# A conditional residual block, item by item: the reaction in a PSUM bank, the identity behind the transposition, and a new order of every engine's slot

## The chip, the cores and the metric

The kernel runs on one core of one Trainium2 chip. The metric is the device time of one execution in microseconds (us). Engines are named as the profile names them: PE is TensorE (PEld its weight loads), DVE VectorE, ACT ScalarE, POOL GpSimd, SP SyncE, which only issues DMAs here.

## The reference

There are 128 items, each a float32 matrix of S = 128 rows and D = 512 columns, and a few numbers per item: a kind (3), a language (10), a category (64), zX, zY, zR. Four residual steps follow one another:

```
scores = tanh(x @ W1 + b1) @ v                      # A = 128 hidden columns
p  = softmax(scores where mask(kind) else -1e30)    # 128 x 128, cnt = allowed columns per row
x1 = x + (p @ x) / cnt
h  = relu(x1 @ W1[lang] + b1[lang]) @ W2[lang] + b2[lang]
x2 = x1 + layernorm(x1 + h) * gamma[lang] + beta[lang]
x3 = x2 + zX*lap_columns(x2) + zY*lap_rows(x2) + zR*x2*(1 - x2)
out = x3 + x3 @ W[cat] + b[cat]
```

`lap` is the second difference with reflected ends, along the columns or along the rows.

## The kernel before, in words

Tables are made first: the items are sorted by category on the chip, so that a category's weights (1 MB, `w3s`, a ring of two places) are fetched only where it changes. Of the 128 fetches 55 are real; for the others the DMA is skipped. Small tables of integers per item (category, is it fresh, place of its weights, item, language, kind) lie in one row, `all_params`; an engine fetches such words into registers with a TENSOR_LOAD (`load_params`, L235).

Then the main loop. Each engine has its own program, written out by hand as slots: slot s does one step of item s, the next step of item s-1, and so on, up to five items apart. Engines meet only at semaphores (`wait_ge`), and each engine takes its instructions in the written order. Every tile of an item has a ring of two. The steps of one item:

- ACT's queue loads the item twice, transposed (`xts`, L565) and plain (`xs`, L572). PE projects the transposed one (`attn_project` L361, `adapter_project` L383); ACT applies tanh (L549); PE makes the scores and adds the mask (L372, L373).
- DVE takes the row maximum (L679), ACT the exponentials and their sum (L502). DVE makes the scale and, at L713, `mix = probs * scale + identity`, so that the residual x1 = x + pooled is one product. PE transposes mix into PSUM (L389), ACT copies it out (`move_mixT`, L524).
- PE: `adapter_hidden` L395, `pool` L402 (x1, into `ps_pool`), ACT: relu L530, PE: `adapter_up` L411 into `ps_adapt`. DVE adds b2 and beta to x1 (L771, L777), sums, centers and normalizes (L686, L692, L722, L746) with ACT's sum of squares (L517) and POOL's inverse deviation (`inverse_std`, L865). L746 writes x2.
- SP copies x2 shifted by one row up and down, with single rows for the reflected ends, through six DMAs inside the on-chip memory (`shift_rows`, L281). POOL adds the two (`sum_rows`, L885) and adds the column neighbours (`sum_columns`, L873; the two ends by ACT, L557).
- Reaction: ACT computes c0 - zR*x2 into the tile `react` (L539), POOL multiplies it by x2 (L879), DVE adds zX times the column sums (`add_columns`, L754) and zY times the row sums (`add_rows`, L764), which gives x3.
- PE transposes x3 in four parts (L419), ACT copies it (L496), PE multiplies by the category's weights (`category`, L429: four blocks of two passes) into `ps_out`, of which there are two banks. POOL adds x3 to the bias (`add_b3`, L892), DVE adds the two (`result`, L739), SP stores it (L272). SP also fetches the weights (L259) and the bias (L267).

PE's slot holds pool, scores, category (its first block, then adapter_up, then the other three), mix_transpose, both projections of the next item, x3_transpose and adapter_hidden. POOL's slot is sum_rows, sum_columns, add_b3, react_times_x2, inverse_std.

Of the kernel before, what the change touches and what calls it, by code (L numbers as in the profile page):

```python
# [12 lines left out]
P = 128  # L13
# [3 lines left out]
CAT, FRESH, WSLOT, ITEM, LANG, KIND, NPARAM = 0, 1, 2, 3, 4, 5, 6  # L17
# [47 lines left out]
def cond_residual_kernel(nc, x, xT, ids, cols, w1a,  # L65
# [22 lines left out]
    with ctx:  # L88
# [71 lines left out]
        react = sb("react", [P, 2, D])  # L160
# [14 lines left out]
        ps_out = [pb("ps_out0"), pb("ps_out1")]  # L175
# [3 lines left out]
        ps_wide = ps_out[0]  # L179
        b2_banks = [ps_out[1], bank_scores]  # L180
# [62 lines left out]
        def _(sp):  # L243
# [31 lines left out]
            def shift_rows(i):  # L275
                q = i.ring(2)
                sp.wait_ge(x2_ready, i.upto())
                for to, at, rows, source in ((below, 0, P - 2, 1), (above, 2, P - 2, 1),
                                             (below, P - 2, 1, P - 1), (below, P - 1, 1, P - 2),
                                             (above, 0, 1, 1), (above, 1, 1, 0)):  # L280
                    sp.dma_start(to[at:at + rows, q], x2[source:source + rows, q]).then_inc(shift_in[q], 16)  # L281

            def slot(s):
# [10 lines left out]
            run_slots(slot, 0, B + 1)  # L294
# [6 lines left out]
        def _(pe):  # L301
# [74 lines left out]
            def adapter_project(s, lang):  # L376
# [3 lines left out]
                if s.is_at_least(2):  # L380
                    pe.wait_ge(relu_ready, s.upto(2))
# [9 lines left out]
            def adapter_hidden(f):  # L391
                if (f + 1).inside(B):
                    pe.wait_ge(xw_ready, (f + 1).upto())
# [28 lines left out]
            def category(j, wslot, ks):  # L422
                if 0 in ks:
                    pe.wait_ge(x3T_ready, j.upto())
                    pe.wait_ge(w3_in[j.ring(2)], j.dma())
                    if j.is_at_least(2):
                        pe.wait_ge(res_ready, j.upto(2))
                for k in ks:
                    mm = pe.matmul(ps_out[j.ring(2)][:, :], x3T[:, j.ring(2), k * P:(k + 1) * P],  # L429
# [3 lines left out]

            def slot(s):
                h, j = s - 1, s - 4
                if h.inside(B):
                    pool(h)
                if s.inside(B):
                    kind, = load_params(pe, KIND, 1, s)
                if j.inside(B):  # L440
                    wslot, = load_params(pe, WSLOT, 1, j)
                if h.inside(B):
                    lang_m1, = load_params(pe, LANG, 1, h)
                if s.inside(B):
                    attn_scores(s, kind)
                if j.inside(B):
                    category(j, wslot, range(0, 1))
                if h.inside(B):
                    adapter_up(h, lang_m1)
                if j.inside(B):  # L450
                    category(j, wslot, range(1, K))
                if (s + 1).inside(B):
                    lang_p1, = load_params(pe, LANG, 1, s + 1)
                if s.inside(B):
                    mix_transpose(s)
                if (s + 1).is_first:
                    attn_project(s + 1)
                    adapter_project(s + 1, lang_p1)
                elif (s + 1).inside(B):
                    adapter_project(s + 1, lang_p1)  # L460
                    attn_project(s + 1)
                if (s - 3).inside(B):
                    x3_transpose(s - 3)
                if s.inside(B):
                    adapter_hidden(s)

            run_slots(slot, -1, B + 3)


        @block.scalar  # L470
        def _(act):
# [48 lines left out]
            def move_mixT(b):  # L520
                act.wait_ge(mixT_mm, b.upto())
                if b.is_at_least(2):
                    act.wait_ge(pool_mm, b.upto(2))
# [423 lines left out]
```

## Time and profile before

| | us |
|---|---|
| three runs | 1098.07, 1097.93, 1093.10 |
| median | 1097.93 |
| the profiled execution, its own time | 1097.21 |
| its span, from the first to the last instruction | 1095.4 |

| engine | busy us | share of the span |
|---|---|---|
| PE | 1055.9 | 96% |
| DVE | 956.5 | 87% |
| POOL | 710.9 | 65% |
| ACT | 504.8 | 46% |

The granted PE clock was 0.998 of full speed. The DMAs moved 268.92 MB, 246 GB/s on average; queue 1 (SP's) took 58.7% of the engines' time and queue 10 (ACT's) 20.4%. A busy share is an average over the run, so it doesn't say what ended a slot; the chain of waits does that for one stretch. "Idle before" of a row is the time that the engine stood still ahead of it, with the engine or DMA that released it.

### The profile page before, as it was taken

How to read it: one execution, taken by the hardware profiler on the slowest of the kernel's cores; microseconds unless marked ns; L12 is line 12 of the kernel's file. 1: busy time of each engine (PE TensorE's matmuls, PEld its weight loads, DVE VectorE, ACT ScalarE, POOL GpSimd, SP SyncE). 2: the span in 40 equal slices, each digit the busy share in tenths (PEclk: the TensorE clock that was granted, in tenths of full speed). 3: DMA queues.
4: the chain of work that ended last, by engine and by line, in shares of the span. 5: the costliest groups of instructions: out<-in, count | busy, mean ns of one | idle time of the engine just before them, and what ended most of it. 6: DMA issues, size and time to landing. Idle time of an engine off the chain costs nothing.

```text
span 1095.4 us, 23744 instructions
## 1 busy us (share of the span) xinstructions
PE 1055.9 (96%) x4912; PEld 656.8 (60%) x4912; DVE 956.5 (87%) x1962; ACT 504.8 (46%) x1422; POOL 710.9 (65%) x665
## 2 busy tenths in 40 slices
PE   6799999999999999999999999999999999999996
PEld 3565666656655656666665566665666565566562
DVE  5799989989989899999888888989898898999994
ACT  3444444444444444445444444444444444444441
POOL 3467667666666676667657666767665766667765
PEclk9999999999999999999999999999999999999999
DMA  8688798678779977876786868887879788897873
GB/s 346 199 260 236 247 293 244 203 250 254 245 230 288 298 239 237 246 229 203 228 266 193 265 198 255 269 266 235 269 241 262 228 268 237 288 276 226 244 241 115
DMA packets 134732, 268.92 MB, mean 246 GB/s; under 512 B 29139, under 2 KB 29157, under 8 KB 127173
## 3 DMA queue, kind: packets, MB, share of 16 engines
q1 hardware_dynamic: 97476, 199.83, 58.7%
q10 hardware_dynamic: 37120, 67.58, 20.4%
q8 instruction: 49, 0.80, 0.3%
q14 instruction: 87, 0.70, 0.2%
HBM read 243.21 MB, written 33.55 MB: 253 GB/s over the span
## 4 chain that ended last, share of the span: by engine, by line
PE 54%; issue 21%; POOL 17%; DVE 6%; DVEq 1%; ACTq 0%; ACT 0%; DMA 0%; POOLq 0%; SPq 0%
PE ps_out L429 23%; POOL b_wide L892 6%; PE ps_adapt L411 6%; PE bank_hidden L383 6%; PE ps_attn L361 6%; PE ps_pool L402 6%; POOL neighbours L873 4%; POOL react L879 3%; PE ps_x3T L419 3%; POOL rstd L865 2%; DVE x L764 2%; PE bank_scores L372 2%; PE bank_hidden L395 1%; DVE res L739 1%; POOL above L885 1%
## 5 line engine op out<-in xcount | busy, mean ns | idle before, releaser
L429 PE MATMUL ps_out<-w3s,x3T 128*128 x1024 | 490.1, 601 | 2.3 <-ACT x3T L496 2.3
L885 POOL TENSOR_TENSOR above<-above,below 128x512 f32<-128x512 f32 x128 | 166.7, 1303 | 226.7 <-DMA above<-x 223.7
L429 PEld LDWEIGHTS ps_out<-w3s,x3T 128*128 128x128 f32 x1024 | 185.1, 191 | 190.6 <-issue 188.7
L764 DVE SCALAR_TENSOR_TENSOR x<-above,wide_rows,react 128x512 f32<-128x512 f32 x128 | 189.5, 1481 | 13.9 <-POOL above L885 12.5
L879 POOL TENSOR_TENSOR react<-react,x 128x512 f32<-128x512 f32 x128 | 175.5, 1371 | 2.4 <-ACT react L539 2.4
L892 POOL TENSOR_TENSOR b_wide<-b_wide,x 128x512 f32<-128x512 f32 x128 | 173.1, 1352 | 1.7 <-DMA b_wide<-in_b 1.7
L865 POOL TENSOR_TENSOR rstd<-var_eps,minus_half 128x1 f32<-128x1 f32 x128 | 70.2, 549 | 132.0 <-DVE var_eps L731 131.9
L517 ACT ACTIVATE square_junk<-ps_adapt,neg_mean 128x512 f32<-128x512 f32 x128 | 88.1, 688 | 139.1 <-DVE neg_mean L692 139.1
L411 PE MATMUL ps_adapt<-w_all,hid 128*128 x256 | 133.0, 601 | 12.6 <-DVE x L746 12.2
L383 PEld LDWEIGHTS bank_hidden<-w_all,xts 128*128 128x128 f32 x1024 | 124.4, 192 | 28.4 <-issue 26.4
L383 PE MATMUL bank_hidden<-w_all,xts 128*128 x1024 | 137.2, 277 | 0.0
L873 POOL TENSOR_TENSOR neighbours<-x 128x510 f32<-128x510 f32 x128 | 133.4, 1042 | 3.6 <-DVE x L746 3.6
L361 PE MATMUL ps_attn<-xts,w_attn 128*128 128x128 f32 x1024 | 135.3, 275 | 0.3 <-issue 0.3
L402 PE MATMUL ps_pool<-xs,mixT 128*128 128x512 f32 x256 | 131.0, 594 | 0.0
L361 PEld LDWEIGHTS ps_attn<-xts,w_attn 128*128 128x128 f32 x1024 | 124.6, 192 | 0.5 <-issue 0.5
L739 DVE TENSOR_TENSOR res<-ps_out,b_wide 128x512 f32<-128x512 f32 x128 | 87.2, 682 | 36.1 <-POOL b_wide L892 26.0
L713 DVE SCALAR_TENSOR_TENSOR mix<-probs,scale,ident 128x128 f32<-128x128 f32 x128 | 108.7, 849 | 0.3 <-issue 0.3
L686 DVE SCALAR_TENSOR_TENSOR ps_adapt<-ps_adapt,x_b 128x512 f32<-128x512 f32 x128 | 89.4, 698 | 17.0 <-PE ps_adapt L411 16.1
L539 ACT ACTIVATE react<-x,c_t,nzr_t 128x512 f32<-128x512 f32 x128 | 102.8, 803 | 2.8 <-DVE x L746 2.8
L502 ACT ACTIVATE probs<-bank_scores,neg_max 128x128 f32<-128x128 f32 x128 | 47.1, 368 | 118.3 <-DVE neg_max L679 118.0
L754 DVE SCALAR_TENSOR_TENSOR react<-neighbours,wide_rows,react 128x512 f32<-128x512 f32 x128 | 96.8, 756 | 0.5 <-POOL react L879 0.5
L722 DVE SCALAR_TENSOR_TENSOR ps_adapt<-ps_adapt,neg_mean,gamma_wide 128x512 f32<-128x512 f32 x128 | 95.5, 746 | 0.1
(111 smaller groups left out, 1281.3 us busy)
## 6 DMA issues: line engine op xcount, KB each, us to landing
w3s<-in_w SPq DMA_DIRECT2D x128, 1024.0 KB
xts<-in_xT ACTq DMA_DIRECT2D x128, 256.0 KB, 4.7
xs<-in_x ACTq DMA_DIRECT2D x128, 256.0 KB, 5.0
b_wide<-in_b SPq DMA_DIRECT2D x128, 256.0 KB, 4.2
out_x<-res SPq DMA_DIRECT2D x128, 256.0 KB, 3.4
below<-x SPq DMA_DIRECT2D x128, 252.0 KB
above<-x SPq DMA_DIRECT2D x128, 252.0 KB
below<-x SPq DMA_DIRECT2D x256, 2.0 KB
```

The source lines that it names most:

```text
L361: mm = pe.matmul(ps_attn, w1_attn[:, k * A:(k + 1) * A], xts[:, r, k, :], start=(k == 0), stop=(k == K - 1))
L383: mm = pe.matmul(ps_xw, xts[:, s.ring(2), k, :], w1_all[:, bass.ds(lang * (K * A) + k * A, A)], start=(k == 0), stop=(k == K - 1))
L402: pe.matmul(ps_pool[:, :], mixT[:, d.ring(2), :], xs[:, d.ring(2), :], start=True, stop=True).then_inc(pool_mm, 1)
L411: pe.matmul(ps_adapt[:, :], hid[:, g.ring(2), :], w2_all[:, bass.ds(lang * D, D)], start=True, stop=True).then_inc(adapt_mm, 1)
L429: mm = pe.matmul(ps_out[j.ring(2)][:, :], x3T[:, j.ring(2), k * P:(k + 1) * P], w3s[:, bass.ds(wslot * (K * D) + k * D, D)], start=(k == 0 ...
L539: nc.scalar.activation(react[:, h.ring(2), :], x2[:, h.ring(2), :], ACT.Identity, bias=c0_t[:, bass.ds(h.n, 1)], scale=nzr_t[:, bass.ds(h. ...
L713: nc.vector.scalar_tensor_tensor(mix[:, p, :], probs[:, p, :], scale[:, p:p + 1], ident[:, :], ALU.mult, ALU.add).then_inc(mix_ready, 1)
L764: nc.vector.scalar_tensor_tensor(x3[:, q, :], above[:, q, :], zy_t[:, bass.ds(i.n, 1)], react[:, q, :], ALU.mult, ALU.add).then_inc(x3_rea ...
L873: nc.gpsimd.tensor_tensor(neighbours[:, q, 1:D - 1], x2[:, q, 0:D - 2], x2[:, q, 2:D], ALU.add).then_inc(neighbours_ready, 1)
L879: nc.gpsimd.tensor_tensor(react[:, q, :], react[:, q, :], x2[:, q, :], ALU.mult).then_inc(react_x2_ready, 1)
L885: nc.gpsimd.tensor_tensor(above[:, q, :], above[:, q, :], below[:, q, :], ALU.add).then_inc(rows_ready, 1)
L892: nc.gpsimd.tensor_tensor(b3_wide[:, q, :], b3_wide[:, q, :], x3[:, q, :], ALU.add).then_inc(x3_b3_ready, 1)
```

## The change

- The reaction is computed in a PSUM bank, `ps_react`, in place of the two-deep tile `react` in on-chip memory. Its product with x2 moves from POOL to DVE.
- `mix = probs * scale` without the identity is now made by ACT (`scale_rows`); the identity is added by DVE while it copies the transposed mix out of PSUM (`add_identity`), which ACT did.
- `ps_out` is one bank, where there were two; the other is `ps_react`. So `category` waits for the `result` of the item before, and ACT's `reaction` for x3 of the item before.
- SP fetches four words per item at once (is it fresh, place, category, item) and keeps them for the later steps; PE, ACT and DVE fetch two at once. The order of the words in the table is changed to suit.
- Every engine's slot has a new order. SP: shift_rows, load_b3 of the item before, store, load_w3. POOL: inverse_std, add_b3, sum_columns, sum_rows.

```diff
-        react = sb("react", [P, 2, D])
-        ps_out = [pb("ps_out0"), pb("ps_out1")]
+        ps_react = pb("ps_react")
+        ps_out = pb("ps_out")
...
 SP
             def slot(s):
                 if s.inside(B):
-                    cat, fresh, wslot = load_params(sp, CAT, 3, s)
+                    words[(s).n] = load_params(sp, FRESH, 4, s)
                     shift_rows(s)
-                    load_w3(s, cat, fresh, wslot)
-                if (s - 2).inside(B):
-                    item_m2, = load_params(sp, ITEM, 1, s - 2)
-                    store(s - 2, item_m2)
-                if s.inside(B):
-                    load_b3(s, cat)
+                if (s - 1).inside(B):
+                    load_b3(s - 1, words[(s - 1).n][2])
+                if (s - 3).inside(B):
+                    store(s - 3, words[(s - 3).n][3])
+                if s.inside(B):
+                    load_w3(s, words[(s).n][2], words[(s).n][0], words[(s).n][1])
...
 ACT
-            def move_mixT(b):
-                act.wait_ge(mixT_mm, b.upto())
-                nc.scalar.activation(mixT[:, b.ring(2), :], ps_mixT, ACT.Copy).then_inc(mixT_ready, 1)
+            def scale_rows(b):
+                act.wait_ge(scale_ready, b.upto())
+                nc.scalar.activation(mix[:, p, :], probs[:, p, :], ACT.Copy, scale=scale[:, p:p + 1]
+                                     ).then_inc(mix_ready, 1)
...
 ACT's slot now: load_x(s-1), scale_rows(s-2), words and load_xT(s), variance(s-3), attn_tanh(s-1),
 relu(s-2), reaction(s-4), exponentials(s-1), move_x3T(s-5), column_ends(s-3), move_xw(s-1)
...
 DVE
-            def mix_rows(b):
-                nc.vector.scalar_tensor_tensor(mix[:, p, :], probs[:, p, :], scale[:, p:p + 1], ident[:, :],
-                                               ALU.mult, ALU.add).then_inc(mix_ready, 1)
+            def add_identity(b):
+                dve.wait_ge(mixT_mm, b.upto())
+                nc.vector.tensor_tensor(mixT[:, b.ring(2), :], ps_mixT, ident[:, :], ALU.add).then_inc(mixT_ready, 1)
+            def react_times_x2(i):
+                dve.wait_ge(react_ready, i.upto())
+                nc.vector.tensor_tensor(ps_react[:, :], ps_react[:, :], x2[:, q, :], ALU.mult).then_inc(react_x2_ready, 1)
...
 DVE's slot now: center(s-2), add_rows(s-4), row_max(s), normalize(s-2), result(s-5), add_b2(s-1),
 denominator(s), row_scale(s), add_adapted(s-1), react_times_x2(s-3), mean(s-1), add_beta(s-1),
 add_identity(s), add_columns(s-3), add_epsilon(s-1)
```

POOL, one slot before. `above` is the sum of the shifted rows, `neighbours` the column sum, `b_wide` the bias sum, `rstd` the inverse deviation; in brackets the semaphores that a row waits for.

```order
L885 TENSOR_TENSOR above<-above,below 128x512 [waits shift_in0]
L873 TENSOR_TENSOR neighbours<-x 128x510 [waits columns_ready,x2_ready]
L892 TENSOR_TENSOR b_wide<-b_wide,x 128x512 [waits b3_in1,x3_ready]
L879 TENSOR_TENSOR react<-react,x 128x512 [waits react_ready]
L865 TENSOR_TENSOR rstd<-var_eps,minus_half 128x1 [waits x2_ready,vareps_ready]
```

The same engine and place now (the last row is the first of the next slot).

```order
L868 TENSOR_TENSOR rstd<-var_eps,minus_half 128x1 [waits x2_ready,vareps_ready]
L889 TENSOR_TENSOR b_wide<-b_wide,x 128x512 [waits b3_in0,x3_ready]
L876 TENSOR_TENSOR neighbours<-x 128x510 [waits columns_ready,x2_ready]
L882 TENSOR_TENSOR above<-above,below 128x512 [waits shift_in0]
L868 TENSOR_TENSOR rstd<-var_eps,minus_half 128x1 [waits x2_ready,vareps_ready]
```

The sum of the shifted rows has moved from the head of the slot to its end, and the product with x2 is gone from this engine.

PE, before: the end of one slot and the start of the next, with the fetches of words (TENSOR_LOAD) ahead of the scores.

```order
L361 MATMUL ps_attn<-xts,w_attn 128x128 x3
L419 MATMUL ps_x3T<-ident,x 128x128 [waits x3T_ready,x3_ready]
L419 MATMUL ps_x3T<-ident,x 128x128 x3
L395 MATMUL bank_hidden<-mixT,xw 128x128 [waits mixT_ready,xw_ready]
L402 MATMUL ps_pool<-xs,mixT 128x512 [waits x1_beta_ready,x_in1]
L235 TENSOR_LOAD all_params x3
L372 MATMUL bank_scores<-attn,v_wide 128x128 [waits mixT_ready,attn_ready]
L373 ISA
L373 MATMUL bank_scores<-masks,ident 128x128
L429 ISA [waits res_ready,w3_in0,x3T_ready]
L429 MATMUL ps_out<-w3s,x3T 128x512
L411 ISA [waits x2_ready,relu_ready]
```

PE now, from adapter_up to the second block of the category product.

```order
L414 REGISTER_ALU [waits x2_ready,relu_ready]
L414 MATMUL ps_adapt<-w_all,hid 128x512
L235 TENSOR_LOAD all_params
L365 MATMUL ps_attn<-xts,w_attn 128x128 [waits attn_ready,xT_in1]
L365 MATMUL ps_attn<-xts,w_attn 128x128 x3
L235 TENSOR_LOAD all_params
L432 ISA [waits res_ready,w3_in0,x3T_ready]
L432 MATMUL ps_out<-w3s,x3T 128x512
L393 MATMUL bank_scores<-ident,mix 128x128 [waits mix_ready]
L432 ISA
L432 MATMUL ps_out<-w3s,x3T 128x512
```

The slot begins with attn_project; one fetch stands ahead of it and one between it and the category product, and the transposition of mix now stands between the first and the second block of that product.

## Rows read from the trace of the kernel before

**Rows 1.** The page, busy time of each engine, share of the span, instructions.

```profile
PE 1055.9 (96%) x4912; PEld 656.8 (60%) x4912; DVE 956.5 (87%) x1962; ACT 504.8 (46%) x1422; POOL 710.9 (65%) x665
```

**Rows 2.** Chain of waits in the stretch 500 to 518: start, length, what.

```profile
500.40 0.22 PE bank_scores L372 x2
...
500.68 0.91 PE ps_out L429 x2
501.59 0.86 PE ps_adapt L411 x2
502.45 2.58 PE ps_out L429 x6
...
505.13 0.89 PE bank_hidden L383 x8
506.03 0.89 PE ps_attn L361 x8
506.92 0.44 PE ps_x3T L419 x4
507.36 0.22 PE bank_hidden L395 x2
507.58 0.86 PE ps_pool L402 x2
```

**Rows 3.** Line L524: ns min/median/max, first and last start in us.

```profile
L524 ACT ACTIVATE mixT<-bank_scores x128: 268/278/278, 25.8 to 1065.3; 128x128 f32<-128x128 f32 x128
```

**Rows 4.** Timeline of ACT near 53 us: start, length, what, idle before.

```profile
52.79 0.28 ACT L524 ACTIVATE mixT<-bank_scores 128x128 f32<-128x128 f32 x1 [0.92 <-PE bank_scores L389]
```

**Rows 5.** Timeline from 268 to 296, a late slot.

```profile
267.84 0.75 DVE L746 SCALAR_TENSOR_TENSOR x<-ps_adapt,rstd,x_beta 128x512 f32<-128x512 f32 x1
...
279.60 1.27 POOL L885 TENSOR_TENSOR above<-above,below 128x512 f32<-128x512 f32 x1 [3.23 <-DMA above<-x]
...
283.67 0.69 DVE L739 TENSOR_TENSOR res<-ps_out,b_wide 128x512 f32<-128x512 f32 x1 [1.22 <-POOL b_wide L892]
...
286.65 1.12 PE L411 MATMUL ps_adapt<-w_all,hid 128*128 x2 [0.20 <-DVE x L746]
```

**Rows 6.** Waits of the whole run: us in total, times, longest.

```profile
POOL above L885 <- DMA above<-x: 223.7, 113, 5.2
```

**Rows 7.** Waits of SP's queue from 60 to 1060.

```profile
SPq L272 <- DVE res L739: 21.0, 31, 2.5
SPq L259 <- PE ps_out L429: 9.4, 20, 0.7
SPq L281 <- DVE x L746: 2.1, 2, 1.1
```

**Rows 8.** The page's groups: busy us, mean ns, idle before and its releaser.

```profile
L764 DVE SCALAR_TENSOR_TENSOR x<-above,wide_rows,react 128x512 f32<-128x512 f32 x128 | 189.5, 1481 | 13.9 <-POOL above L885 12.5
L879 POOL TENSOR_TENSOR react<-react,x 128x512 f32<-128x512 f32 x128 | 175.5, 1371 | 2.4 <-ACT react L539 2.4
...
L739 DVE TENSOR_TENSOR res<-ps_out,b_wide 128x512 f32<-128x512 f32 x128 | 87.2, 682 | 36.1 <-POOL b_wide L892 26.0
L713 DVE SCALAR_TENSOR_TENSOR mix<-probs,scale,ident 128x128 f32<-128x128 f32 x128 | 108.7, 849 | 0.3 <-issue 0.3
```

**Rows 9.** Line L764: ns min/median/max.

```profile
L764 DVE SCALAR_TENSOR_TENSOR x<-above,wide_rows,react x128: 737/1750/1766, 44.1 to 1083.4; 128x512 f32<-128x512 f32 x128
```

**Rows 10.** Line L235 on SP's queue, whole run.

```profile
L235 SPq TENSOR_LOAD <-all_params x256: 277/612/2469, 17.7 to 1086.2; - x128
```

**Rows 11.** Tile xts, all 128 loads.

```profile
DMA to landing us min/median/max: 2.7/4.7/7.8
```

**Rows 12.** Tile xs, all 128 loads.

```profile
DMA to landing us min/median/max: 3.1/5.0/9.5
```

**Rows 13.** Timeline near the end: x2 of the last item.

```profile
1074.01 0.75 DVE L746 SCALAR_TENSOR_TENSOR x<-ps_adapt,rstd,x_beta 128x512 f32<-128x512 f32 x1
```

**Rows 14.** Line L235 on PE's queue, from 499 to 509.

```profile
L235 PEldq TENSOR_LOAD <-all_params x6: 302/307/565, 498.8 to 507.3; - x6
```

More of the change, by code:

```diff
@@ L432, in category @@
                     mm.then_inc(out_mm, 1)
+            words = {}
             def slot(s):
-                h, j = s - 1, s - 4
-                if h.inside(B):
-                    pool(h)
                 if s.inside(B):
[L439 to L443, printed above, removed]
-                if s.inside(B):
-                    attn_scores(s, kind)
@@ L446, in slot @@
[L446 to L453, printed above, removed]
-                if s.inside(B):
[L455 to L461, printed above, removed]
@@ L462, in slot @@
-                if (s - 3).inside(B):
-                    x3_transpose(s - 3)
-                if s.inside(B):
-                    adapter_hidden(s)
-            run_slots(slot, -1, B + 3)
+                    words[(s).n] = load_params(pe, LANG, 2, s)
+                    attn_project(s)
+                if (s - 5).inside(B):
+                    wslot, = load_params(pe, WSLOT, 1, s - 5)
+                    category(s - 5, wslot, range(0, 1))
+                if (s - 1).inside(B):
+                    mix_transpose(s - 1)
@@ new lines, in slot @@
+                if (s - 5).inside(B):
+                    category(s - 5, wslot, range(1, K))
+                if (s - 1).inside(B):
+                    adapter_hidden(s - 1)
+                if s.inside(B):
+                    attn_scores(s, words[(s).n][1])
+                if (s - 1).inside(B):
+                    pool(s - 1)
+                if (s - 4).inside(B):
+                    x3_transpose(s - 4)
+                if s.inside(B):
+                    adapter_project(s, words[(s).n][0])
@@ L470, in _ @@
+                if (s - 1).inside(B):
+                    adapter_up(s - 1, words[(s - 1).n][0])
+            run_slots(slot, 0, B + 4)
         @block.scalar
@@ L572, in load_x @@
                 act.dma_start(xs[:, r], x[bass.ds(item, 1)].rearrange("o s d -> s (o d)")).then_inc(x_in[r], 16)
+            words = {}
             def slot(s):
+                if (s - 1).inside(B) and not (s - 1).is_first:
+                    load_x(s - 1, words[(s - 1).n][0])
+                if (s - 2).inside(B):
+                    scale_rows(s - 2)
+                if s.inside(B):
+                    words[(s).n] = load_params(act, ITEM, 2, s)
+                    load_xT(s, words[(s).n][0])
+                if s.is_first:
+                    load_x(s, words[s.n][0])
+                    for i in range(4, L):
+                        move_b2(i)
+                if (s - 3).inside(B):
+                    variance(s - 3)
+                if (s - 1).inside(B):
+                    attn_tanh(s - 1)
+                if (s - 2).inside(B):
+                    relu(s - 2, words[(s - 2).n][1])
+                if (s - 4).inside(B):
+                    reaction(s - 4)
@@ L602, in slot @@
-                if (s - 1).inside(B):
-                    lang_m1, = load_params(act, LANG, 1, s - 1)
-                    relu(s - 1, lang_m1)
-            run_slots(slot, -1, B + 3)
+                if (s - 1).inside(B):
+                    move_xw(s - 1)
+            run_slots(slot, 0, B + 4)
         @block.vector
```

140 lines of the change are left out of this document (59 added, 81 removed).

## The prediction

> **What bounds the kernel now.** I began with the page's line of busy times [rows 1]: TensorE is busy for 1055.9 of 1095.4 us, VectorE for 956.5, GpSimd for 710.9, ScalarE for 504.8. Divided by 128 items that is 8.25, 7.47, 5.55 and 3.94 us. Such shares don't say what ends a slot, so next came the chain of waits over one slot in the middle [rows 2]. It holds matmuls alone: 0.22, 0.91, 0.86, 2.58, 0.89, 0.89, 0.44, 0.22 and 0.86 us, and between them two short pieces (the mask, 0.06, and the transpose of mix, 0.11) whose rows are left out; from 500.40 to 507.58 + 0.86 it is 8.04 us. There TensorE is the bound, and no order of the same matmuls gives a shorter slot than 8.04.
>
> Third, how often a slot is that short. The copies of the transposed mix run from 25.8 to 1065.3, and the fifth starts at 52.79 [rows 3, 4]. So 123 slots take 1012.5 us, 8.23 each; at 8.04 they would take 988.9. That leaves 23.6 us of stalls, plus a start-up (four gaps in 27.0 us, 6.75 each) and the end.
>
> Fourth, where the stalls come from [rows 5 to 7]. Item i's x2 was ready at 268.59; the sum of the shifted rows (L885) started at 279.60, 11.0 us later, after 3.23 us of waiting for the shift DMAs. That sum is the first of GpSimd's five instructions in a slot, so the column sum, the bias sum, the product and the inverse deviation all stood behind it. VectorE's res waited 1.22 us for the bias sum; everything behind it on VectorE came late, x2 among it, and L411 waited for x2 at 286.65. Over the run L885 waited 223.7 us, at worst 5.2 [rows 6]. The shifts are late partly because SP, which issues them, hardly ever rests: between 60 and 1060 it waited 21.0 + 9.4 + 2.1 = 32.5 us [rows 7]. The rest, 967.5 of 1000, or 7.96 per slot of 8.23, is its own issuing. SP is a second bound, just under TensorE's 8.04.
>
> **The change, part by part.** *Engine sums.* GpSimd loses L879: 1.37 us (175.5 by 128) [rows 8], 5.55 - 1.37 = 4.18. VectorE gains that product: one operand in PSUM, one in SBUF, 128x512, as in L739, 0.68. Its last sum (L764) took 1.48 on average and between 0.74 and 1.77 singly [rows 8, 9]; I take 0.74. L713 (0.85) gives way to add_identity, 128x128 out of PSUM. No such row exists on VectorE: from below 0.28, ScalarE's copy of that shape [rows 3], from above the 0.85 of L713 itself; I take 0.28, since 0.85 is a mean of an instruction with both operands in SBUF, and the new one has one. Sum: 7.47 + 0.68 - 0.74 - 0.57 = 6.84, and with the upper ends (1.48, 0.85) 8.15, which would be over 8.04.
>
> Behind the 0.74: L739, with one input in PSUM, averages 0.68 beside the same GpSimd work; L764, with both in SBUF, is the one that stretches. The Trainium skill's page "SBUF — State Buffer" (section "Who interferes with whom") says that a VectorE instruction with at most one SBUF input doesn't contend with GpSimd. By that rule L764's successor takes 0.74; if it stayed stretched, VectorE's sum would be 7.58. Both are below 8.04, so the slot stays the same.
>
> *One slot in the new order*, zero at attn_project(s), durations from rows 2: projection to 0.89, first category part 1.8, transpose of mix(s-1) 1.9, category 4.45, hidden 4.67, scores 4.95, pool(s-1) 5.8, x3 transposes 6.25, adapter_project 7.15, adapter_up(s-1) 8.0. VectorE starts at 4.95 with the maximum; x2(s-2) is ready at 5.95, result(s-5) at 6.6, add_b2 7.25, the scale 7.55; it waits for adapter_up until 8.0, then add_adapted 8.85, product 9.5, add_beta 10.25, identity 10.5, columns 11.2, center 12.0, rows 12.7, and waits for the next scores at 12.99. (Durations on VectorE: 0.68 and 0.74, 0.15 to 0.3 for the narrow ones.) It idles 0.45 and 0.3. Margins of TensorE's waits: x2(s-2) 5.95 against 7.15; x3(s-4) 12.7 - 8.04 = 4.7 against 5.8; relu(s-1) about 5.1 against 6.25; mix(s-1), now scaled by ScalarE, about 7.95 against 8.04 + 1.8; the single category bank, read by 6.6 - 8.04, against 0.89. None is under 1.1 us, so the single banks (category, reaction) cost nothing in a regular slot. The cover of the category bank is the 4.4 us of other matmuls between two category products; without it result's 2.2 us (scores to 6.6, a half us more) would show in every slot.
>
> *Late shifts.* x2(i) is ready in slot i+2 at 5.95; its rows are added in slot i+4 from 12.0 - 8.04 = 3.96 on. That is 14.1 us, less 1.3 for the sum: the DMAs may take 12.8, where 11.0 already stalled before. And L885's successor now stands last in GpSimd's slot, so what waits behind it is the next inverse deviation. The worst wait was 5.2, 2 us beyond the 3.23 of that case, so some 13: a few slots will still lose a little.
>
> *SP.* One of its two TENSOR_LOADs per item goes, median 0.61 us [rows 10]: 7.96 - 0.61 = 7.35. The new one fetches four words for three; how that costs no row tells. From one side nothing, from the other the whole 0.61 back; I take nothing, since ends are near and both stay below 8.04. The new order puts store behind shifts and b3, where res is long done, so the 21.0 us of that wait go too; w3 waits for out_mm as before.
>
> *The input xT.* Here a margin shrinks. xT(s+1) is issued at about 7.85 (behind x and the scaled rows), once adapter_project has read its half of the ring, and is wanted 8.2 us later. Landings of xT are 2.7 to 7.8 us, median 4.7; those of x, which now stands just ahead of xT as xT stood ahead of x, 3.1 to 9.5, median 5.0 [rows 11, 12]. I give xT the landings of x: a few over 8.2, 3 us in all (from 0; to 1.3 each if every one met x's worst, which is a rival below). The page "DMA: Bandwidth & Descriptors" of the Trainium skill (section "Queues, rings and completion order") says that descriptors of one ring are consumed in ring order; by it xT can't begin before x's descriptors, which is the direction taken here.
>
> *Start and end.* Five of TensorE's fill slots hold 8.04 - 3.49 - 0.44 = 4.1 us of matmuls; before, their gaps were 6.75 because the mix ran through VectorE behind other work. I estimate 5.4 and a first one 1.4 later (xT(1) is issued a slot later): 4 us less, from 0 to 8. At the end mix(127) to x2(127) was 1074.75 - 1065.3 = 9.5 [rows 3, 13]; by the slot above it is 9.8. The 20.6 us from there to the end (shifts, sums, transpose, category, store) are the same chain: 0, give or take 3.
>
> *Sum.* 1095.4 - 23.6 + 6 (3 for xT, 3 for shifts and SP) - 4 + 0.3 = 1074.1 span. The profiled execution took 1097.21, 1.8 more than its span, and stands 0.7 under the median of the runs: 1074.1 + 2.5 = 1076.6, said as 1076.
>
> **Rivals.** *A sequencer gap (slower).* The WSLOT load now follows attn_project, whose eight passes are short, and category waits behind the load. If TensorE's sequencer reached it only as the last pass starts, each slot would show the load, 0.30 us [rows 14]: 128 x 0.3 = 39, so 1076 + 39 = 1115. It decides once 0.17 us per slot shows (21 us of gain by 128). Against it: loads run ahead. The six between 498.8 and 507.3 include those for the scores of the next slot, which begin at 508.44, and there is no gap before them [rows 2]; in the new slot the last wait ahead, x2 at 5.95, is 1.2 us before the array needs it. 8%.
>
> *xT paces the slots (slower).* The ring closes a loop over two slots: 7.15 to adapter_project's end, 0.7 to issue, then the landing L: slot = (7.85 + L) / 2. It decides from L = 8.23, and passes before's 8.23 per slot at 8.6. With x's worst, 9.5, on every item it is 8.68: 128 x 0.64 = 82, so 1158. For it: two loads adjacent on one queue, and denser traffic. Against: median 5.0. 6%.
>
> *The stalls stay.* If shifts are late because the DMAs are full, and the four-word load takes what two took, SP remains at 7.96 and catches up nothing; stalls go on at 16 to 24 us and only the start is won: 1098 - 4 - 4 = 1090. For it: SP waits 3% only, and stalls come in clusters. Against: two more us of tolerance, and a place in the order where a late sum holds up one tiny instruction. 15%.
>
> **Numbers.** Forecast 70%, own range 1064 to 1088; stalls stay 15%; gap 8%; xT 6%; 1% elsewhere. 0.5% (5.5 us) is about what a measurement of this kernel can tell from no change: faster is below 1092.4. Faster: 0.69 + 0.09 = 0.78. Same: 0.01 + 0.05 + 0.01 (a small gap) = 0.07. Slower: 0.15. Range 1062 to 1098: it leaves out the two slower rivals and a little on either side of the rest.
>
> **What would show it.** Right: nearly all slots of 8.04, a chain of matmuls alone in mid-run; the rows sum still waiting for its DMAs with no res or L411 behind it; VectorE's rows sum at 0.74 always. Wrong: TensorE idle before category with "issue" (the gap), before attn_project with a DMA (xT), before adapter_up with x2 (a VectorE chain I summed too short). If the slots are 8.04 and the time is off by over 5 us, start or end was mis-sized.

## The result, and the profile after

| | before | after |
|---|---|---|
| median of the paired runs, us | 1096.87 (1093.1 to 1098.07) | 1116.32 (1112.42 to 1120.93) |
| ratio after / before, 95% interval | | 1.0185 [1.015, 1.0221] |
| span of the profiled execution, us | 1095.4 | 1112.2 |

The changed kernel is 1.9% slower. 1076 was forecast, and 1098 was the upper end of the range. The first lines of the page after stand against [rows 1]: busy time, then the chain's shares.

```profile
PE 1063.5 (96%) x4912; PEld 657.2 (59%) x4912; DVE 872.8 (78%) x2090; ACT 499.3 (45%) x1422; POOL 530.0 (48%) x537
...
PE 73%; DMA 19%; ACTq 2%; SPq 2%; issue 1%; ACT 1%; DVE 1%; POOL 0%; DVEq 0%; POOLq 0%
```

VectorE and GpSimd lost what they were to lose, and 19% of the chain is now a DMA. Which one, the page's groups say (busy us, mean ns, idle before and its releaser), to be held against [rows 6, 8]:

```profile
L882 POOL TENSOR_TENSOR above<-above,below 128x512 f32<-128x512 f32 x128 | 162.3, 1268 | 99.1 <-DMA above<-x 98.9
...
L365 PEld LDWEIGHTS ps_attn<-xts,w_attn 128*128 128x128 f32 x1024 | 132.0, 192 | 96.7 <-DMA xts<-in_xT 54.9
...
L365 PE MATMUL ps_attn<-xts,w_attn 128*128 128x128 f32 x1024 | 139.4, 280 | 25.0 <-DMA xts<-in_xT 24.4
...
L765 DVE SCALAR_TENSOR_TENSOR x<-above,wide_rows,ps_react 128x512 f32<-128x512 f32 x128 | 94.7, 740 | 3.2 <-POOL above L882 3.2
```

TensorE's weight loads stood 54.9 us in front of `attn_project`, waiting for xT (its matmuls 24.4 beside them, which overlap and don't add). The chain of waits around 500 us shows such a slot and the start of the next, at 511.14 (start, length, what; compare [rows 2]):

```profile
495.81 6.86 DMA xts<-in_xT
502.66 0.04 issue
502.71 1.16 PE ps_attn L365 x8
503.87 0.98 PE ps_out L432 x2
504.85 0.11 PE bank_scores L393
504.95 2.58 PE ps_out L432 x6
507.53 0.22 PE bank_hidden L398 x2
507.75 0.22 PE bank_scores L376 x2
...
508.03 0.92 PE ps_pool L405 x2
508.95 0.44 PE ps_x3T L422 x4
509.38 0.89 PE bank_hidden L387 x8
510.28 0.86 PE ps_adapt L414 x2
511.14 0.89 PE ps_attn L365 x8
512.03 0.86 PE ps_out L432 x2
```

Where nothing is late the slot is 8.04 (503.87 to 512.03 is 8.16, the 0.12 being the slow end of the late one), with no gap ahead of `category`. Reading the start of every `attn_project` from the timeline: item 5 at 54.17, item 127 at 1070.44, so 122 slots took 35.4 us more than 8.04 each. 27.3 of these lie in 36 slots whose projection starts within 0.3 us of xT's landing, and in all 36 a real weight fetch had been issued in the 8 us before that load. One such fetch, in the timeline (start, length, what):

```profile
532.04 0.35 SPq L259 DMA_DIRECT2D w3s<-in_w  x1
...
534.52 0.34 ACTq L571 DMA_DIRECT2D xs<-in_x  x1
...
536.20 0.34 ACTq L564 DMA_DIRECT2D xts<-in_xT  x1
```

and the DMA view after it, a window 532.5 to 537.5 and one 537.5 to 544 (queue 1 is SP's, 10 is ACT's; packets, MB, share of 16 engines):

```profile
q1 hardware_dynamic: 273, 1.13, 77.7%
...
q1 hardware_dynamic: 734, 1.27, 60.4%
q10 hardware_dynamic: 308, 0.57, 26.3%
```

In the first window no packet of ACT's queue moved. ACT had asked for nothing in its first 2 us; x was asked for at 534.52, and its first packet started at 538.0. xT landed 7.7 us after its issue, 11.9 after the fetch. Over the run xT, issued within 8 us behind such a fetch, landed after a median of 7.3 us (54 loads; 28 took longer than the 7.25 us that there were, which the section on the failed step derives); otherwise after 4.0 (74 loads, none over 7.25). The median over all hides that there are two kinds (compare [rows 11]):

```profile
DMA to landing us min/median/max: 2.6/4.6/8.8
```

### The profile page after: what moved, and what is told of

It reads as the page before. It is cut to its first block, busy times and chain, and to the rows that moved or that the text cites. A ratio compares the mean times of both kernels' runs of the same rounds, so it can differ in the third digit from the quotient of the medians.

```text
span 1112.2 us, 23107 instructions
## 1 busy us (share of the span) xinstructions
PE 1063.5 (96%) x4912; PEld 657.2 (59%) x4912; DVE 872.8 (78%) x2090; ACT 499.3 (45%) x1422; POOL 530.0 (48%) x537
## 4 chain that ended last, share of the span: by engine, by line
PE 73%; DMA 19%; ACTq 2%; SPq 2%; issue 1%; ACT 1%; DVE 1%; POOL 0%; DVEq 0%; POOLq 0%
PE ps_out L432 31%; DMA xts<-in_xT 18%; PE ps_attn L365 9%; PE ps_pool L405 8%; PE bank_hidden L387 8%; PE ps_adapt L414 6%; PE ps_x3T L422 4%; PE bank_scores L376 2%; PE bank_hidden L398 2%; ACTq L235 1%; SPq L283 1%; PE bank_scores L393 1%; ACT mix L522 1%; ACTq L571 1%; PE bank_scores L377 1%
## 5 line engine op out<-in xcount | busy, mean ns | idle before, releaser
L432 PE MATMUL ps_out<-w3s,x3T 128*128 x1024 | 479.4, 598 | 5.2 <-DVE res L735 2.2
L432 PEld LDWEIGHTS ps_out<-w3s,x3T 128*128 128x128 f32 x1024 | 176.4, 192 | 170.3 <-issue 169.7
L882 POOL TENSOR_TENSOR above<-above,below 128x512 f32<-128x512 f32 x128 | 162.3, 1268 | 99.1 <-DMA above<-x 98.9
L365 PEld LDWEIGHTS ps_attn<-xts,w_attn 128*128 128x128 f32 x1024 | 132.0, 192 | 96.7 <-DMA xts<-in_xT 54.9
L529 ACT ACTIVATE hid<-bank_hidden,vals 128x128 f32<-128x128 f32 x128 | 47.0, 367 | 296.1 <-PE bank_hidden L398 296.1
L889 POOL TENSOR_TENSOR b_wide<-b_wide,x 128x512 f32<-128x512 f32 x128 | 162.7, 1271 | 3.5 <-DMA b_wide<-in_b 2.6
L365 PE MATMUL ps_attn<-xts,w_attn 128*128 128x128 f32 x1024 | 139.4, 280 | 25.0 <-DMA xts<-in_xT 24.4
L422 PEld LDWEIGHTS ps_x3T<-ident,x 128*128 128x128 f32 x512 | 63.7, 141 | 70.3 <-issue 63.6
L677 DVE TENSOR_REDUCE neg_max<-bank_scores 128x1 f32<-128x128 f32 x128 | 37.3, 291 | 84.6 <-PE bank_scores L377 84.4
L538 ACT ACTIVATE ps_react<-x,c_t,nzr_t 128x512 f32<-128x512 f32 x128 | 99.3, 776 | 6.4 <-DVE x L765 6.1
L765 DVE SCALAR_TENSOR_TENSOR x<-above,wide_rows,ps_react 128x512 f32<-128x512 f32 x128 | 94.7, 740 | 3.2 <-POOL above L882 3.2
L755 DVE SCALAR_TENSOR_TENSOR ps_react<-neighbours,wide_rows,ps_react 128x512 f32<-128x512 f32 x128 | 95.7, 747 | 0.1
L742 DVE SCALAR_TENSOR_TENSOR x<-ps_adapt,rstd,x_beta 128x512 f32<-128x512 f32 x128 | 95.0, 742 | 0.3 <-issue 0.2
```

The costliest lines, as they stand in the source:

```text
L365: mm = pe.matmul(ps_attn, w1_attn[:, k * A:(k + 1) * A], xts[:, r, k, :], start=(k == 0), stop=(k == K - 1))
L422: mm = pe.transpose(ps_x3T[:, k * P:(k + 1) * P], x3[:, i.ring(2), k * P:(k + 1) * P], ident[:, :])
L432: mm = pe.matmul(ps_out[:, :], x3T[:, j.ring(2), k * P:(k + 1) * P], w3s[:, bass.ds(wslot * (K * D) + k * D, D)], start=(k == 0), stop=(k ...
L538: nc.scalar.activation(ps_react[:, :], x2[:, h.ring(2), :], ACT.Identity, bias=c0_t[:, bass.ds(h.n, 1)], scale=nzr_t[:, bass.ds(h.n, 1)]). ...
L755: nc.vector.scalar_tensor_tensor(ps_react[:, :], neighbours[:, q, :], zx_t[:, bass.ds(i.n, 1)], ps_react[:, :], ALU.mult, ALU.add).then_in ...
L882: nc.gpsimd.tensor_tensor(above[:, q, :], above[:, q, :], below[:, q, :], ALU.add).then_inc(rows_ready, 1)
```

## The experiments

Differences in us between runs of different groups are taken from the ratios, times 1095. The last two columns are read from each trace: us over 8.04 per slot between `attn_project` of items 5 and 127, and the start of that of item 5. A trace is one execution, whose time can stand away from the median of its row: spo's took 1099.70 us, w1's 1112.24, kb's 1087.44. So these two columns explain that execution, and the ratio says what the edit is worth.

| run | median us | ratio to before, 95% | over 8.04 | item 5 at |
|---|---|---|---|---|
| changed kernel | 1116.32 | 1.0185 [1.015, 1.0221] | 35.4 | 54.17 |
| r3_ring_of_three | 1074.01 | 0.9794 [0.9753, 0.9834] | 0.5 | 51.23 |
| ox_xT_before_x | 1081.75 | 0.9859 [0.9826, 0.9892] | 5.5 | 53.75 |
| w1_words_early | 1108.03 | 1.0092 [1.0056, 1.0128] | 34.5 | 56.1 |
| st_xT1_first | 1112.58 | 1.0137 [1.0096, 1.0178] | 40.7 | 49.34 |
| nf_after | 1077.89 | 0.9838 [0.9794, 0.9883] | | |
| nf_before | 1076.94 | 0.9829 [0.9785, 0.9873] | | |
| spo_sp_order_before | 1089.86 | 0.9956 [0.9922, 0.999] | 20.8 | 54.3 |
| b_pool_rows_late | 1114.47 | 1.0168 [1.0123, 1.0212] | | |
| sd_shifts_2us_later | 1118.78 | 1.0197 [1.0147, 1.0247] | | |
| oxsp_xT_first_sp_before | 1084.84 | 0.987 [0.9822, 0.9918] | 7.4 | 54.34 |
| r3_react_in_sbuf | 1091.22 | 0.9943 [0.9906, 0.998] | | |
| b_r3_ring_in_before | 1094.9 | 0.9999 [0.9965, 1.0032] | | |
| kb_b3_behind_fetch | 1089.99 | 0.9963 [0.9936, 0.9989] | 9.8 | 53.06 |
| ks_store_behind_fetch | 1088.59 | 0.9947 [0.9924, 0.9969] | 7.6 | 56.56 |
| kk_both_behind_fetch | 1103.5 | 1.008 [1.0052, 1.0108] | 23.6 | 55.59 |

**r3_ring_of_three.** xT gets a third place, and is asked for a slot earlier.

```diff
-        xts = sb("xts", [P, 2, K, S])
+        xts = sb("xts", [P, 3, K, S])
-            load_xT(s)        # waits for the readers of item s-2
+            load_xT(s + 1)    # waits for the readers of item s-2
```

> The changed kernel with a third place in the ring of xts, and xT(s+1) issued in ACT's slot s (behind the same wait as xT(s) had), so each load has one slot (8.04 us) more. Theory A (late xT: the 35 slots that wait for xT cost 27.1 us, and xT(1) behind the b2 copies costs the start some 8): both go, 1114 - 27 - 7 = about 1080, no PE wait for DMA xts left. Theory B (the traffic itself is slower in the new order, xT only shows it first): the wait moves to another transfer, w3, x or the shifts, and the time stays above 1100.

1074.01, the fastest kernel of this study, 2.1% under before. xT still lands after 7.4 us behind a fetch, but TensorE doesn't wait for it. The page's chain and the projection:

```profile
PE 95%; SPq 2%; DVE 1%; issue 1%; DMA 1%; ACTq 0%; ACT 0%; POOL 0%; DVEq 0%; POOLq 0%
...
L365 PE MATMUL ps_attn<-xts,w_attn 128*128 128x128 f32 x1024 | 136.8, 277 | 0.0
```

The span is 39.3 below the changed kernel's: 2.9 at the start (51.23 against 54.17), 34.9 in the slots, 1.5 behind item 127's projection (40.3 against 41.8). So the waits for xT are the loss, including the 8.1 us that my rule of 0.3 us didn't ascribe to them. With xT in time the change gives 1074, 2 below what was forecast for it.

**ox_xT_before_x and w1_words_early.** Two ways to ask earlier. w1 fetches the words in the slot before; ox does that and also issues xT ahead of x and of the scaled rows.

```diff
 w1: words(s+1) fetched behind attn_tanh(s-1)
 ox: w1, and
-            load_x(s-1); scale_rows(s-2); load_xT(s)
+            load_xT(s); load_x(s-1); scale_rows(s-2)
```

> The changed kernel with ACT's words fetched in the middle of the slot before, and xT issued ahead of x and of the scaled rows. Theory A: xT is issued about 1.2 us earlier (slot - 0.4 for slot + 0.8), and no longer stands behind x, so behind a real w3 fetch it lands in 5.5 us as before the change, for 7.3: nearly no wait for xT in regular slots, 1114 - 27 = about 1087. Theory B: landings behind a w3 fetch stay at 7.3 or more whatever stands ahead on ACT's queue; with 8.4 us of room some 10 us are won, 1104.

> The changed kernel with only ACT's words fetched in the middle of the slot before; x still stands ahead of xT. It prices the two-word load (0.70 us median on ACT's queue) in front of xT. Theory A: xT is issued at slot + 0.1 for + 0.8, landings stay 7.3 behind a w3 fetch, each of the 35 waits is some 0.6 us shorter, 20 us less: about 1094. If the order of x and xT is all that counts: 1110 or more.

w1 missed: by the ratios it won 10 us, give or take 5, where theory A gave it 20. xT was issued 0.7 us earlier in the slot (0.10 instead of 0.80 behind attn_project's start) and its landing grew by 1.0, to 8.3 behind a fetch. From the fetch's issue to xT's landing it is 11.4, against 11.6. So the landing time is no constant to be added to the issue.

ox met the time of theory A (1087, 1081.75 measured) but not its mechanism: xT landed 7.9 us after its issue, as theory B had it, and not 5.5. It was issued so much earlier that 8.5 us were left, and it landed 10.4 behind the fetch. With xT ahead, x landed 11.7 behind the fetch; with x ahead, in the changed kernel, x landed after 10.2 and xT after 11.6. Of ACT's queue the first load asked for lands first.

This agrees with the Trainium skill, "DMA: Bandwidth & Descriptors", section "Queues, rings and completion order", by which descriptors of one ring are consumed in ring order.

**st_xT1_first.** xT(1) is issued in slot 0, ahead of the b2 copies.

```diff
+                    words[1] = load_params(act, ITEM, 2, s + 1)
+                    load_xT(s + 1, words[1][0])
                     for i in range(4, L):
                         move_b2(i)
```

> The changed kernel with only xT(1) issued ahead of ACT's copies of b2, in slot 0. It prices the start alone: PE waited 3.23 us for xT(1) at 28 us and then ran at a granted clock of 0.57 until 36. Theory A: both go, attn_project(5) comes 5 to 8 us sooner, about 1107. If the start's clock falls for another reason: 3 us less at most, 1111.

The start got 4.8 us shorter, and the granted clock stayed at 1.00 throughout. The median, 1112.58, is nearer to the second expectation. In the changed kernel TensorE stood waiting for xT(1) for 3.23 us; behind that, its windows read as follows (us, busy of PE, PEld, DVE, ACT, POOL with counts, granted clock, DMA share, GB/s):

```profile
21.90:28.20 6.30, 2.62 (x19) 2.25 (x19) 0.94 (x4) 1.50 (x5) 0.00 (x0) 1.00 0.93 360
28.20:36.20 8.00, 7.50 (x26) 5.51 (x27) 1.56 (x5) 1.76 (x6) 0.00 (x0) 0.57 0.06 22
```

The second is a clock near the lower of the two levels (0.5), for 8 us. That the wait for xT(1) alone makes it isn't shown: in r3, where xT(1) also comes early and TensorE's longest wait between 10 and 20 us was 0.95, the granted clock was 0.50 from 20 to 28 us. In the kernel before, the same stretch kept its clock:

```profile
20.50:28.20 7.70, 5.99 (x44) 5.17 (x45) 1.65 (x6) 2.29 (x8) 0.00 (x0) 1.00 0.87 343
28.20:36.20 8.00, 5.32 (x28) 3.22 (x26) 5.87 (x17) 3.73 (x12) 1.70 (x3) 1.00 0.41 121
```

In the traced executions hardly anything of the 4.8 us is left at item 127 (1070.96 against 1070.44), since the slots took 5.3 us more; the end was 2.7 shorter. By the ratios the edit won 5 us, give or take 6. So whether a head start is waited away where a DMA paces the slots isn't shown: slots of one kernel differ as much from one execution to the next.

**nf_after and nf_before.** The flag for a fresh category is held at zero from item 9 on, so 52 of the 55 fetches don't happen, and the later products use stale weights.

> The changed kernel with the real fetches of category weights left out from the ninth item on (3 of 55 remain, the later products use stale weights). Theory A (xT arrives when the 1 MB fetch ahead of it and x have drained): xT lands in about 4.1 us everywhere, no wait for it: 1114 - 35 = about 1079, only the slow start stays. Theory B (xT is late because of its place on ACT's queue, with or without a fetch): waits shrink little, over 1100.

> The kernel before with the same fetches left out from the ninth item on. If its 23.6 us of stalls come from shift DMAs delayed by the fetches: all gone, 1095 - 22 = about 1073. If SP's own issuing (7.96 us per slot) makes them: at least half stays, 1083 or more.

Both near what was expected (1079 and 1073), and the rivals, over 1100 and 1083 or more, are out. The waits of TensorE's weight loads for xT fell from 54.9 to 4.6 us. The stalls of the kernel before came from the fetches too, by another way (late shifts: 223.7 us of waiting, 123.2 without the fetches). Without them the two kernels are within 0.1% of each other, so where no fetch disturbs the slots the change wins nothing. The chains read, of after and of before:

```profile
PE 93%; SPq 2%; DMA 2%; DVE 1%; issue 1%; ACT 0%; ACTq 0%; POOL 0%; DVEq 0%; POOLq 0%
```

```profile
PE 95%; DVE 2%; issue 1%; POOL 1%; DMA 0%; DVEq 0%; ACT 0%; SPq 0%; POOLq 0%
```

**spo_sp_order_before.** The changed kernel with SP's old order.

```diff
-  shift_rows(s); load_b3(s-1); store(s-3); load_w3(s)
+  shift_rows(s); load_w3(s); store(s-2); load_b3(s)
```

> The changed kernel with SP's order of before (shifts, w3, store, b3) and its fetch of four words. Theory A (x ahead of xT and the late issue decide, SP's order does not): xT still lands 11 to 12 us after a real fetch is issued, time within 8 us of 1114. Theory B (w3 straight ahead of the shifts is what stretches the landings): xT lands 9.4 us after the fetch as before, the waits go, about 1085.

1089.86: theory B for the most part. SP's order is worth 25 us of the changed kernel's time, give or take 5 (1.0185 - 0.9956). Behind a fetch xT lands 9.9 us after the fetch was issued, against 11.6, and after 6.8 of its own, against 7.3. But the waits didn't go, as theory B had it: in the traced execution, one of the two slowest of ten, they are still 41.7 us.

The edit does more than reorder. It stores item s-2 for s-3, and that store waits for res (89.1 us, 97 times, from 60 to 1060). So the next shifts are issued 3.0 us after x2 instead of 0.2, and 3.4 us behind a real fetch instead of 1.4.

**sd_shifts_2us_later** tests whether the shifts close behind the fetch are what is in xT's way.

```diff
             def shift_rows(i):
+                sp.wait_ge(adapt_mm, (i + 1).upto())
```

> The changed kernel with SP's shifts of item i held until adapter_up of item i+1 is done, some 2 us after x2(i); SP's order else unchanged. Theory C (xT comes late because the shift DMAs are issued straight behind a real weight fetch, 1.2 us after it, and hold the DMA engines while x and xT should pass): with 3.3 us between fetch and shifts, as in the order of before, xT lands about 10 us after the fetch for 11.6, the waits for xT go, about 1090 though shifts start later. Theory D (store and bias load ahead of the fetch for behind it make the difference): xT still lands 11.5 us after the fetch, 1114 or slower.

1118.78, with the waits for xT longer than the 54.9 of the changed kernel. But the run doesn't rule theory C out. Held shifts also held up the fetch behind them, which was issued 6.2 us into the slot instead of 5.0, so the distance to the next shifts was 2.2 us and not the 3.3 that were meant. xT did arrive sooner behind the fetch, 10.6 for 11.6, near the 10 of theory C and not at the 11.5 of theory D; the later fetch took that back, and xT landed 8.2 us after its own issue.

```profile
PEld ps_attn L367 <- DMA xts<-in_xT: 67.2, 51, 5.1
```

**kb, ks, kk.** What is left of the order are the bias and the store, 256 KB each, which stand between the shifts and the fetch.

```diff
 kb
-  load_b3(s-1); store(s-3); load_w3(s)
+  store(s-3); load_w3(s); load_b3(s-1)
 ks
+  load_b3(s-1); load_w3(s); store(s-3)
 kk
+  load_w3(s); load_b3(s-1); store(s-3)
```

> The changed kernel with one edit on SP: load_b3(s-1) is issued behind load_w3(s), no longer ahead of shift's successor, so SP's slot is shifts, store, w3, b3. The bias broadcast is 256 KB of the 512 KB that stand ahead of the 1 MB fetch. Theory D1 (the bias ahead of the fetch is what makes xT late): w3 is issued about 0.7 us earlier in the slot, xT lands within 6.8 behind a fetch instead of 7.3, arrives about 10 us after it instead of 11.6, waits of attn_project for xT fall from 54.9 us to below 30, time 1095 to 1104. Theory D2 (the store ahead of the fetch is): 1111 to 1117 as the changed kernel. Theory D3 (only bytes count, whichever DMA they belong to): about half way, 1100 to 1106, here and in the run with the store moved.

> The changed kernel with one edit on SP: store(s-3) is issued behind load_w3(s), so SP's slot is shifts, b3, w3, store. Theory D2 (the store of 256 KB ahead of the fetch makes xT late): waits of attn_project for xT below 30 us, 1095 to 1104. Theory D1 (the bias): 1111 to 1117. Theory D3 (bytes): 1100 to 1106.

> The changed kernel with SP's slot as shifts, w3(s), b3(s-1), store(s-3): both behind the fetch, items as in the changed kernel. Theory D (what stands ahead of and behind the fetch): as with the SP order of the kernel before, 1086 to 1094, xT landing 6.8 behind a fetch, fetch issued 5.8 into the slot or earlier, and fewer than 25 slots that wait for xT. If the time stays over 1105, it was not the place of b3 and the store that made 1116 of 1090 but the item they are issued for (b3 of the item before, the store one slot later).

Each alone brings 24 to 26 us (1089.99, 1088.59), more than any theory gave it; both together only 12 (1103.5), where 1086 to 1094 was expected. The 14 us between kk and spo, which has both behind the fetch too, hang on the items that bias and store are issued for and on the store's wait. Waits of TensorE's weight loads for xT, first of kb, then ks, then kk (us, times, longest):

```profile
PEld ps_attn L365 <- DMA xts<-in_xT: 28.3, 43, 3.5
```

```profile
PEld ps_attn L365 <- DMA xts<-in_xT: 28.1, 38, 5.3
```

```profile
PEld ps_attn L365 <- DMA xts<-in_xT: 49.1, 50, 5.0
```

The fetch is issued 5.0 us into the slot in all four, since it waits there for `category`'s last read (91 to 104 us of waiting on SP from 60 to 1060). From its issue to xT's landing: 11.6 with 512 KB ahead of it, 10.8 and 10.6 with 256 KB on either side, 11.3 with 512 KB behind. So neither D1, D2 nor "bytes ahead" holds. Two readings are left, and no run separates them. One is that what stands ahead delays the fetch's end, and what stands behind shares the DMA engines with x and xT. The other is theory C again: each transfer moved behind the fetch also moves the next shifts away from it, to 1.8 us in kb, 2.0 in ks and 2.5 in kk, against 1.4. With 3.4, in spo, xT came after 9.9, though there too 512 KB stood behind the fetch. What in SP's order makes xT late stays open; that SP's order does it is shown.

Nor do the medians say what a run loses: behind a fetch xT's own landing is 6.9 in both kb and kk, while the slots lost 9.8 and 23.6. The late ones do the harm: one load in ten behind a fetch took over 7.5 in kb and over 7.9 in kk.

**oxsp_xT_first_sp_before.** ox and spo together.

> The changed kernel with xT ahead of x (words fetched a slot ahead) and SP's order of before (shifts, w3, store, b3), ring of two. If both add up, xT lands some 9 us after the fetch, no wait for it: the slots are all 8.04 as with the ring of three, 1114 - 35 = about 1078. If they are one effect: no better than 1082.

No better than ox (1084.84; 1081.75), though xT landed 8.1 us after the fetch and held up one slot alone. What TensorE's matmuls waited for between items 5 and 127 is the transposition's input `mix`, which ScalarE makes here behind both loads (7 of the 8 waits of the first row). The other two rows are the sum of the shifted rows and, from 60 to 1060 us, SP's store:

```profile
PE bank_scores L393 <- ACT mix L522: 4.7, 8, 0.9
...
POOL above L885 <- DMA above<-x: 216.9, 112, 4.7
...
SPq L272 <- DVE res L738: 82.6, 90, 1.9
```

Its 216.9 us are near the 223.7 of [rows 6]: the shifts are late again, but they end no slot here, since VectorE waited for that sum only twice, for 6.2 us together. What brings them back seems to be the store's wait for res rather than the place of the fetch: spo waits 209.0 us for shifts, and kk, with the fetch in the same place and the store an item older, 93.4, against 98.9 in the changed kernel.

**b_pool_rows_late** puts only the row sum behind the product in the kernel before.

```diff
-  POOL: sum_rows, sum_columns, add_b3, react_times_x2, inverse_std
+  POOL: sum_columns, add_b3, react_times_x2, sum_rows, inverse_std
```

> The kernel before with one edit: POOL's sum of the shifted rows moved from the head of the slot behind the product with x2. If the stalls of before come from late shifts that hold up the rest of POOL's slot: most of 23.6 us go, about 1078. If they come from SP's or the DMAs' limit: within 5 us of 1095.

A miss, 1114.47. GpSimd still had the product ahead of the sum, and VectorE's row addition now had to wait for it in 126 of 128 items. Nearly every slot became 8.33:

```profile
DVE x L764 <- POOL above L885: 155.4, 126, 2.5
```

Alone, the late row sum does harm. The run says nothing on the changed kernel, where that wait is 3.2 us.

**r3_react_in_sbuf** takes the PSUM reaction back out of r3.

```diff
+        react_sb = sb("react_sb", [P, D])      # in place of ps_react
```

> The kernel with the ring of three, and the reaction in one tile of on-chip memory instead of the PSUM bank. Its product and both sums then have two operands in the memory that POOL shares. Theory (the PSUM operand spares VectorE the stretch beside POOL, but TensorE covers it): the sum of the rows takes 1.3 to 1.7 us for 0.74, VectorE is busy 7.4 to 7.8 us per item for 6.8, time within 6 us of 1074. Rival (VectorE becomes the bound): over 1085.

1091.22, 16 us over r3. I had expected at most 6. The same line in r3 and in this run:

```profile
L768 DVE SCALAR_TENSOR_TENSOR x<-above,wide_rows,ps_react 128x512 f32<-128x512 f32 x128 | 94.5, 738 | 7.6 <-issue 5.1
```

```profile
L769 DVE SCALAR_TENSOR_TENSOR x<-above,wide_rows,react_sb 128x512 f32<-128x512 f32 x128 | 182.6, 1426 | 1.5 <-issue 1.0
...
PE 58%; issue 15%; POOL 13%; DVE 9%; ACTq 2%; ACT 1%; DVEq 1%; DMA 0%; POOLq 0%; SPq 0%
```

The same instruction takes 1426 ns with all operands in SBUF and 738 with one in PSUM. VectorE's sum stays below 8.04 (7.62), as the prediction argued, but x3 comes late: ACT's reaction waited for it 88 times and TensorE's x3 transposes 92. The reaction has one buffer in both kernels, so its longer use shows in full; how much a second buffer would hide wasn't run.

```profile
ACT react_sb L539 <- DVE x L769: 60.3, 88, 4.6
...
PEld ps_x3T L423 <- DVE x L769: 65.8, 92, 2.3
```

**b_r3_ring_in_before** gives the kernel before the third place.

> The kernel before with the same third place for xts and xT issued a slot earlier. Control: xT had 7 us to spare there, so nothing is to be won but in the start, 1090 to 1097. If a deeper prefetch helps whatever the order is (by thinning the traffic), 1080 or less.

Ratio 0.9999: before, xT held up nothing, and a ring of three alone is worth nothing.

## Why the prediction was wrong

The step that failed is "I give xT the landings of x: a few over 8.2, 3 us in all". It cost 27.3 us by the strictest count, 34.9 by r3, where 3 were forecast. Three things in it were wrong.

- *The landings.* The median of 4.7 [rows 11] is over a mixture, 54 loads behind a real fetch and 74 not. Split, before reads 5.5 and 4.2 for xT, and x, issued later behind the same fetch, 5.9 and 4.7. The longest of [rows 11], 7.8, was nearer to what the changed kernel met (7.3 behind a fetch) than the median.
- *The order of SP's queue.* I priced it in SP's own time and in the store's wait (correctly: SP was busy 1000 - 104.0 - 14.8 = 881 us between 60 and 1060, 7.33 per slot, where 7.35 was forecast). I gave it no price in what it does to the arrivals on ACT's queue. spo, kb and ks each show that price to be about 25 us, give or take 5; by which way is open, as said there.
- *The window.* I had xT issued at 7.85 with 8.2 us to go. The trace has it 0.80 behind the start of attn_project, 8.84 on my clock, which leaves 7.25. ACT's two-word fetch is part of that: 700 ns, where its fetches in the kernel before took 281.

```profile
L235 ACTq TENSOR_LOAD <-all_params x128: 485/700/2549, 14.1 to 1061.8; - x128
```

```profile
L235 ACTq TENSOR_LOAD <-all_params x384: 272/281/1155, 13.5 to 1066.2; - x192
```

(The first is of after, the second of before; ns min/median/max.) A window of 7.25 and a landing of 7.3 behind a fetch: the margin was gone in just those slots.

The rival "xT paces the slots" named the right wait, with 6%. Its condition, L of 8.23, rests on the same 7.85; with 8.84 it is 7.24, and 28 of the 54 loads behind a fetch took longer. So it held there alone, and in no slot without a fresh fetch.

The other steps, in order:

- *Slots of 8.04:* right, in r3 (0.5 us over in 122 slots) and in the changed kernel wherever nothing is late. No gap ahead of `category`; the sequencer rival was wrong.
- *VectorE:* 872.8 / 128 = 6.82, forecast 6.84. L765 takes 0.740 in every item (736 to 747 ns), where L764 took up to 1766 [rows 9]; the rule of the Trainium skill's page "SBUF — State Buffer" (section "Who interferes with whom") holds. *add_identity* 0.28, as taken. *GpSimd:* 530.0 / 128 = 4.14, forecast 4.18.
- *Late shifts:* right. The waits for them fell from 223.7 to 98.9 and held up VectorE twice, for 3.2 us together. The shifts also wait for x3 of the item two before, which the diff leaves out; no wait of SP between 60 and 1060 was for it.
- *SP's fetch of words:* the 0.61 of [rows 10] is a median over two kinds as well, 0.96 for three words and 0.45 for one. The four words took 0.92. By these medians 0.49 went, by the means 0.75 (1.57 to 0.81 per item), where 0.61 was taken.
- *Start:* the forecast sum puts the fifth copy of the transposed mix, now L710, at 52.79 - 4 = 48.8; it is at 56.28, 7.5 late. In it are the 3.23 us of waiting for xT(1) and the clock's fall. My "a first one 1.4 later" left out that xT(1) stands behind the b2 copies on ACT's queue.
- *End:* 31.1 us from the last such copy (1081.0), forecast 1095.4 - 1065.3 + 0.3 = 30.4.

So the 38.1 us between forecast and measured span are 7.5 at the start, 35.8 - 6 = 29.8 in the slots (35.8 over 8.04 in the 123 from that fifth copy to the last) and 0.7 at the end. In r3, which takes the failed step away, the same three are 4.6, -5.5 and -0.3: its 1074 agrees with the forecast partly because two misses cancel.

## What to carry to other kernels

A landing time is not a property of a load. Split it by what is in flight on the other queues, and for a load that moves closer to its use, compare the window with the landings beside the largest transfer, not with the median of all. An order of DMA issues has two prices, the issuing engine's time and what it does to the arrivals on other queues; the second was the greater here. Moving one issue also moves those behind it, so an experiment on the order has to say which distances it changed. If a load's tolerance shrinks through a reorder, another buffer is the first thing to try: here it turned 1116 into 1074.

## What the hardware showed that I had not expected

- A real 1 MB fetch on SP's queue delayed a 256 KB load on ACT's queue in two parts. Over the loads of x whose queue was idle at their issue, the first packet came 2.2 us after the issue behind a fetch (38 loads, longest 3.6) and 1.1 otherwise (45 loads); from the first packet to the landing it took 5.2 against 3.1. So more of the delay lies in the time when both queues move packets. The windows from 534.5 to 538 (no packet of queue 10) and from 538.2 to 541.5, behind the fetch shown above:

```profile
q1 hardware_dynamic: 145, 0.80, 75.0%
...
q1 hardware_dynamic: 344, 0.60, 56.9%
q10 hardware_dynamic: 226, 0.42, 39.5%
```

  The Trainium skill ("DMA: Bandwidth & Descriptors", "Queues, rings and completion order") has each engine take turns between the queues by packets. The second window agrees with that, as far as counts over all engines can show it. What holds up the first packet isn't shown.
- Words fetched together are not always free. A fetch of two on ACT took 700 ns against 281 for one; on SP, four took 918 against 962 for three and 448 for one. VectorE still fetches one word in the changed kernel, not two as the section on the change has it, in 310 ns against 311 before.
- A wait of 3.2 us by TensorE near the start was followed by 8 us at a granted clock of 0.57; r3 had 8 us at 0.50 without such a wait.
- Moving two 256 KB transfers behind the fetch gained less than moving either of them.
